# A DRAM scratch laid out chunk by chunk, and tiles re-paired so that each partition's copy is one run

## What is computed

```python
x0 = xk = e                                   # (B, 39, 16), e from 39 gathers
for idx, (W, b) in enumerate([(w0, b0), (w1, b1), (w2, b2)]):
    z = jnp.einsum('bhd,bkd,hks->bsd', x0, xk, W) + b[None, :, None]
    z = jax.nn.relu(z)                        # (B, 128, 16)
    if idx != 2:
        xk = z[:, :64, :]; direct.append(z[:, 64:, :])
    else:
        direct.append(z)
logit = jnp.sum(jnp.concatenate(direct, axis=1), axis=-1)
h = jnp.concatenate([logit, dense_ctx], axis=1)
h = relu(h @ W_top1 + b_top1); h = relu(h @ W_top2 + b_top2); y = h @ W_top3
```

## Time and profile before

| | us |
|---|---|
| median of 3 runs | 2626.11 |
| lowest and highest | 2624.89, 2628.14 |
| span of the profiled execution | 2627.2 |
| PE busy | 2462.9 (94%) |
| DVE busy | 2273.2 (87%) |
| POOL busy | 1559.0 (59%) |
| ACT busy | 1176.3 (45%) |
| SP's DMA queue, share of 16 engines | 88.7% |

### The profile page before, as it was taken

How to read it: one execution, slowest core, us unless ns; L and a number is a source line. 1 busy time by engine, 2 the same in 40 slices (tenths; PEclk the granted TensorE clock), 3 DMA queues, 4 the chain that set the end, 5 groups by cost and what they waited for, 6 DMA issues and landing times.

```text
span 2627.2 us, 25816 instructions
## 1 busy us (share of the span) xinstructions
PE 2462.9 (94%) x7712; PEld 1439.5 (55%) x7712; DVE 2273.2 (87%) x1356; ACT 1176.3 (45%) x1414; POOL 1559.0 (59%) x1030
## 2 busy tenths in 40 slices
PE   0399999999999999999999999999999999999999
PEld 0155555555555555555555555555555555555553
DVE  0389989898998999899999989999898999989970
ACT  0144444444444444444444444444444444444442
POOL 6456666576666656665765666566566656732340
PEclk9899999999999999999999999999999999999999
DMA  2999999999999999999999999999999999999920
GB/s 61 182 200 201 200 185 197 193 193 186 200 198 188 194 192 199 189 194 196 191 196 186 202 190 194 193 194 195 184 200 185 198 194 197 194 187 196 194 47 0
DMA packets 262599, 477.02 MB, mean 182 GB/s; under 512 B 19371, under 2 KB 37675, under 8 KB 262501
## 3 DMA queue, kind: packets, MB, share of 16 engines
q1 hardware_dynamic: 242102, 471.34, 88.7%
q0 software_dynamic: 20480, 5.47, 1.7%
HBM read 468.99 MB, written 7.74 MB: 181 GB/s over the span
## 4 chain that ended last, share of the span: by engine, by line
PE 67%; POOL 10%; issue 7%; DMA 6%; DVE 6%; ACT 2%; SPq 1%; POOLq 0%; DVEq 0%; ACTq 0%
PE z L647 34%; PE z L670 29%; POOL emb L339 5%; DMA emb<-in_tbl,idx 5%; DVE prod L406 4%; POOL pair_lo L210 4%; PE xk L729 1%; DMA x_pairs<-x_transposed 1%; PE z L729 1%; ACT pair_hi L520 1%; PE turned L628 1%; POOL half_parts L206 1%; DVE logit L436 1%; DVE pair_lo L210 1%; ACT direct L581 0%
## 5 line engine op out<-in xcount | busy, mean ns | idle before, releaser
L406 DVE TENSOR_TENSOR prod<-x_pairs,xk 128x2048 f32<-128x2048 f32 x640 | 1439.5, 2282 | 142.3 <-PE z L670 107.0
L647 PE MATMUL z<-prod,w_plain 128*128 128x512 f32 (+2 forms) x2944 | 1401.5, 600 | 48.7 <-issue 27.0
L520 ACT CAST pair_hi<-prod 128x1024 fp32r<-128x1024 f32 x703 | 735.5, 1046 | 1122.3 <-PE z L670 780.6
L210 POOL TENSOR_TENSOR pair_lo<-prod,pair_hi 128x1024 fp32r<-128x1024 f32 x320 | 763.5, 2386 | 679.3 <-ACT pair_hi L520 663.9
L647 PEld LDWEIGHTS z<-prod,w_plain 128*128 128x128 f32 (+2 forms) x2944 | 561.6, 191 | 488.6 <-issue 407.7
L339 POOL DMA_INDIRECT emb<-in_tbl,idx x624 | 702.2, 1125 | 189.3 <-issue 176.6
L670 PE MATMUL z<-pair_hi,w_lo 128*128 128x512 f32 (+1 forms) x1408 | 793.2, 563 | 2.6 <-DVE pair_lo L210 1.7
L670 PE MATMUL z<-pair_lo,w_hi 128*128 128x512 f32 (+1 forms) x1408 | 556.8, 395 | 0.0
L670 PE MATMUL z<-pair_hi,w_hi 128*128 128x512 f32 (+1 forms) x1408 | 556.1, 395 | 0.0
L210 DVE TENSOR_TENSOR pair_lo<-prod,pair_hi 128x1024 fp32r<-128x1024 f32 (+1 forms) x384 | 468.1, 1219 | 49.5 <-ACT pair_hi L520 48.7
L670 PEld LDWEIGHTS z<-pair_hi,w_lo 128*128 128x128 f32 (+1 forms) x1408 | 267.0, 190 | 300.4 <-POOL pair_lo L210 139.9
(11 more groups left out here) (50 smaller groups left out, 567.0 us busy)
## 6 DMA issues: line engine op xcount, KB each, us to landing
x_pairs<-x_transposed SPq DMA_DIRECT2D x128, 2432.0 KB
x_diag<-x_transposed SPq DMA_DIRECT2D x192, 546.0 KB
x_pairs<-x_transposed SPq DMA_DIRECT2D x64, 256.0 KB
x_diag<-x_transposed SPq DMA_DIRECT2D x192, 78.0 KB
emb<-in_tbl,idx POOLq DMA_INDIRECT x624
x_transposed<-stage SPq DMA_DIRECT2D x32, 156.0 KB
x_transposed<-stage SPq DMA_DIRECT2D x32, 80.0 KB
x_pairs<-in_w SPq DMA_DIRECT2D x2, 704.0 KB, 7.0
```

The costliest lines, as they stand in the source:

```text
L210: engine.tensor_tensor(pair_lo[0:rows, pair % PAIR_RING], held[0:rows, at:at + 2, :], pair_hi[0:rows, pair % PAIR_RING].bitcast(F32), ALU. ...
L406: nc.vector.tensor_tensor(prod[0:rows, pos % RING, 0:n, :], a, xk.unsqueeze(1).broadcast_to([rows, n, N]), ALU.mult).then_inc(prod_ready, 1)
L520: nc.scalar.copy(pair_hi[0:rows, pair % PAIR_RING], held[:, at:at + 2, :]).then_inc(hi_ready, 1)
L647: ins = nc.tensor.matmul(z[n][:], w, held[0:rows, i, :], start=(k == 0 and i == plain[0]), stop=(k == last_slot and not here and i == plai ...
```

## The change

- The scratch becomes `[64 chunks, 59 x 512]`: a row is a chunk, and in it the fields stand one behind the other, 2 KB each, 118 KB in all. The store has the same shapes and piece sizes (1 KB).
- `x0_diag`: band i, tile t, partition f holds field f + 7i + t, in place of f + 3t + i. A partition's seven pieces are now one run of 14 KB.
- `x0_pairs`: tile t holds field t on partitions 0 to 63 and field t + 19 on 64 to 127. Each partition's 19 pieces are one run of 38 KB.
- The weights are paired to match. The host function is the same text, but with other constants (`DIAG` 1, `T0` 21, `PLAIN_TILES` 0 to 18) it lays `w0` out as 39 rows of 21 tiles and `w1`, `w2` as 20 tiles in their natural order. SP picks the halves: layer 0's two arrays with three DMAs each, layers 1 and 2 with one DMA per half tile (64 partitions x 128 values, 512 bytes a partition), and one each for the last tile.

```diff
-    xt = nc.dram_tensor("x0_transposed", [F + WRAP, COLS], F32, kind="Internal").ap()
+    xt = nc.dram_tensor("x0_transposed", [GROUPS * CHUNKS, (F + WRAP) * N], F32, kind="Internal").ap()
...
-            sp.dma_start(w0_swapped, w0s).then_inc(swapped_in, 16)
-            sp.dma_start(w0_raw, w0f).then_inc(swapped_in, 16)
-            plain = [len(PLAIN_TILES[n]) for n in (1, 2)]
-            for raw, w, first in zip(w_raw[1:], (w1, w2), plain):
-                sp.dma_start(raw.rearrange("p (t s) -> p t s", s=S), w[:, first:]).then_inc(raw_in, 16)
-            loads = [(w_plain[1][:], w1[:, 0:plain[0]]), (w_plain[2][:], w2[:, 0:plain[1]]),
...
+            for dst, src in ((w0_swapped, w0s), (w0_raw, w0f)):
+                for i in range(BANDS):
+                    sp.dma_start(dst[i * F:(i + 1) * F], src[:, i * TILES0 * S:(i + 1) * TILES0 * S]
+                                 ).then_inc(swapped_in, 16)
+            def load_rows(dst, w, tiles, loaded):
+                for half in range(2):
+                    rows = slice(half * HALF, (half + 1) * HALF)
+                    for at, t in enumerate(tiles):
+                        h = t + half * (TX - 1)
+                        sp.dma_start(dst[rows, at], w[h % 2 * HALF:(h % 2 + 1) * HALF, h // 2]
+                                     ).then_inc(loaded, 16)
+            for raw, w, n in zip(w_raw[1:], (w1, w2), (1, 2)):
+                raw = raw.rearrange("p (t s) -> p t s", s=S)
+                load_rows(raw, w, SPLIT[n], raw_in)
+                sp.dma_start(raw[:, W_SPLITS[n] - 1], w[:, TX - 1]).then_inc(raw_in, 16)
+            for dst, w, n in zip(w_plain[1:], (w1, w2), (1, 2)):
+                load_rows(dst[:], w, PLAIN[n], weights_in)
+            sp.dma_start(columns[:], small).then_inc(weights_in, 16)
...
-                    shifted = bass.AP(tensor=chunk.tensor, offset=chunk[i:i + F].offset,
-                                      ap=[[COLS, F], [DIAG * COLS, T0], [1, N]])
-                    sp.dma_start(x0_diag[rows, 0:T0, :], shifted).then_inc(x0_diag_in, 16)
+                    shifted = bass.AP(tensor=chunk.tensor, offset=chunk[:, i * TILES0 * N:].offset,
+                                      ap=[[N, F], [1, TILES0 * N]])
+                    sp.dma_start(x0_diag[rows, 0:TILES0, :].rearrange("p t n -> p (t n)"), shifted
+                                 ).then_inc(x0_diag_in, 16)
...
-                    src = chunk[half:half + F - 1].rearrange("(t two) n -> t two n", two=2)[:, 0, :]
-                    sp.dma_start(buf[half * HALF:(half + 1) * HALF, 0:TX - 1, :],
-                                 src.partition_broadcast(HALF)).then_inc(loaded, 16)
+                    src = chunk[:, half * (TX - 1) * N:(half + 1) * (TX - 1) * N]
+                    sp.dma_start(buf[half * HALF:(half + 1) * HALF, 0:TX - 1, :]
+                                 .rearrange("p t n -> p (t n)"),
+                                 src.rearrange("o n -> (o n)").partition_broadcast(HALF)
+                                 ).then_inc(loaded, 16)
```

More of the change, by code:

```diff
@@ L49 @@
 RING = 4
-SL0, SLX = -(-T0 // QUAD), TX // QUAD
+SL0, SLX = -(-TILES0 // QUAD), TX // QUAD
 SLC = SL0 + 2 * SLX
-L0_FIRST = range(0, T0, QUAD)
+L0_FIRST = range(0, TILES0, QUAD)
 FIRST_TILE = (0, 4, 16, 8, 12)
@@ L66 @@
 assert CHUNKS * sum(PAIRS.values()) % PAIR_RING == 0
-SPLIT_TILES = {n: [(FIRST_TILE if n else L0_FIRST)[k] + at + i
+SPLIT = {n: [(FIRST_TILE if n else L0_FIRST)[k] + at + i
                    for k, at, m in SPLITS[n] for i in range(m) if m == 2] for n in SPLITS}
-PLAIN_TILES = {n: [t for t in range(TX - 1 if n else T0) if t not in SPLIT_TILES[n]] for n in SPLITS}
+PLAIN = {n: [t for t in range(TX - 1 if n else TILES0) if t not in SPLIT[n]] for n in SPLITS}
 W_ORDER = (1, 2, 0)
-W_SPLITS = {n: len(SPLIT_TILES[n]) + (n > 0) for n in SPLITS}
-X0_DIAG_DMAS, X0_PAIRS_DMAS, ST_DMAS = 2 * DIAG, 3, 4
-RAW_DMAS, WEIGHT_DMAS, TOP_DMAS = 2, 3, 6
+DIAG, T0, R0 = 1, BANDS * TILES0, F
+PLAIN_TILES = {n: list(range(TX - 1)) for n in (1, 2)}
+SPLIT_TILES = {n: [] for n in (1, 2)}
+W_SPLITS = {n: len(SPLIT[n]) + (n > 0) for n in SPLITS}
+X0_DIAG_DMAS, X0_PAIRS_DMAS, ST_DMAS = 2 * BANDS, 3, 4
+TOP_DMAS = 6
+RAW_DMAS = sum(2 * len(SPLIT[n]) + 1 for n in (1, 2))
+WEIGHT_DMAS = sum(2 * len(PLAIN[n]) for n in (1, 2)) + 1
 H1, H2, DENSE = 512, 256, 16
@@ L130, in build @@
         ident = sb("ident", [P, P])
-        w_plain = [sb(f"w{n}_plain", [P, len(PLAIN_TILES[n]), S]) for n in SPLITS]
+        w_plain = [sb(f"w{n}_plain", [P, len(PLAIN[n]), S]) for n in SPLITS]
         w_hi = [sb(f"w{n}_hi", [P, W_SPLITS[n], S], F32R) for n in SPLITS]
@@ L201, in low_part @@
         def low_part(engine, layer, pos, at, n, pair):
-            held, rows = prod[:, pos % RING], P if layer else R0
+            held, rows = prod[:, pos % RING], P if layer else ROWS0
             if n == 1:
@@ L248, in load_chunk @@
             def load_chunk(bt, c):
-                first = ahead(bt * (P * D) + c * N)
+                first = ahead(bt * CHUNKS + c)
                 sums = bt * CHUNKS + c
@@ L261, in load_chunk @@
                     sp.wait_ge(summed2, sums)
[L262 to L263 removed]
+                chunk = xt[bass.ds(first, 1), :]
+                base = chunk[:, 0:F * N].rearrange("o (f n) -> (o f) n", n=N)
+                for i in range(BANDS):
                     rows = slice(i * F, (i + 1) * F)
[L266 to L269 removed]
+                    shifted = bass.AP(tensor=chunk.tensor, offset=chunk[:, i * TILES0 * N:].offset,
+                                      ap=[[N, F], [1, TILES0 * N]])
+                    sp.dma_start(x0_diag[rows, 0:TILES0, :].rearrange("p t n -> p (t n)"), shifted
+                                 ).then_inc(x0_diag_in, 16)
+                    sp.dma_start(x0_diag[rows, TILES0, :], base).then_inc(x0_diag_in, 16)
                 if not (isinstance(bt, int) and bt == c == 0):
@@ L416, in products @@
                         dve.wait_ge(xk0_ready, next_chunk + 1)
-                    first, rows, tiles = (FIRST_TILE[k], P, TX) if n else (L0_FIRST[k], R0, T0)
+                    first, rows, tiles = (FIRST_TILE[k], P, TX) if n else (L0_FIRST[k], ROWS0, TILES0)
                     product(slot, pos, copies[0:rows, first:min(first + QUAD, tiles), :], xk[0:rows])
@@ L640, in layer @@
                     here = [s for s in splits if s[0] == k]
-                    places = range(QUAD if n else min(QUAD, T0 - t))
+                    places = range(QUAD if n else min(QUAD, TILES0 - t))
                     plain = [i for i in places if not any(at <= i < at + m for _, at, m in here)]
@@ L644, in layer @@
                     for i in plain:
-                        rows = P if n else R0_LAST if t + i == T0 - 1 else R0
-                        w = whole[0:rows, PLAIN_TILES[n].index(t + i), :]
+                        rows = P if n else ROWS0_LAST if t + i == TILES0 - 1 else ROWS0
+                        w = whole[0:rows, PLAIN[n].index(t + i), :]
                         ins = nc.tensor.matmul(z[n][:], w, held[0:rows, i, :],
@@ L661, in layer @@
                             for i in range(2):
-                                j = SPLIT_TILES[n].index(t + at + i)
-                                rows = P if n else R0
+                                j = SPLIT[n].index(t + at + i)
+                                rows = P if n else ROWS0
                                 p_hi = pair_hi[0:rows, pair % PAIR_RING, i, :]
```

37 lines of the change are left out of this document (15 added, 22 removed).

## The result

| | before | after |
|---|---|---|
| median, us | 2625.5 (4 runs, 2623.77 to 2628.14) | 2928.95 (4 runs, 2920.93 to 2934.69) |
| ratio | | 1.1155, 95% interval 1.1129 to 1.1182 |
| span of the profiled execution | 2627.2 | 2932.9 |
| mean granted clock | 0.982 | 0.949 |

The account below looks back on a forecast made before the run. PE was taken as the bound, with DMA costing time only in the start and at 15 group turns, through gathers behind x0 loads. 2627.2 - 21 - 72 = 2534, less 1.1 to the median, 2533 us; range 2524 to 2615, chance 0.79.

Parts of the forecast that it names:

- I take 395, the row of long runs: x0 loads: with runs of 14 and 38 KB they would move at 395 GB/s, like the weights.
- The lower bound, 205: x0 loads: the lowest rate allowed for, 205 GB/s, meaning no change.
- Part 2: Group turns: x0_pairs is in before the last gather, so PE's wait and clock dip go; 4.8 x 15 = 72 us gained.
- Part 1: Start: the first chunk's loads come in sooner; 21 us gained, bounds 0 and 23, up to 5 more for the clock.
- the 2 us that I gave ACT's "remote" wait: Start: ACT's wait, taken as a fetch sharing the DMA engines that ends when they are free, given 2 us.
- layer 0's copies were to be in at 76.0: Start: layer 0's 1872 KB at 395 GB/s would be in at 76.0, so layer 0 is no obstacle.
- Part 3: Start: 85 weight DMAs on SP take 39 us, covered by the gathers until 60.5; at 1.04 each, 26 us lost.
- I take 0.45, near the small one: Start: SP's time per small weight DMA, 0.45 us, so 39 us for all 85.
- Part 4: Store pieces, padding, DVE's products and matmuls keep their shapes: no effect on the time.
- Rival 4: Group turns: gathers starve behind 38 KB pieces, 3.0 us each; PE waits 4 us longer 15 times; 2686 us, chance 0.15.
- Rival 3: Start and turns: nothing changes, since reading one place from 16 engines is the limit; 2626 us, chance 0.06.
- rivals 1 and 2: x0 loads: rate rises partway, 250 GB/s, 2583 us, chance 0.15; only piece overhead goes, +4.7%, 2609 us, chance 0.06.

Follow-up runs that it names:

- e5: Kernel before, with x0_pairs read in 2 KB pieces from an embedding table, each of the 64 partitions from its own place: 2616.32 us.
- e6: Kernel before, with x0_pairs read in 2 KB pieces from an embedding table, all 64 partitions reading the same 19 pieces: 2628.70 us.
- e1: Changed kernel, with 256 B of nothing behind each field in the scratch, so that copies are 2 KB pieces again: 2643.84 us.
- e15: Kernel before, its two x0_pairs DMAs writing even and odd partitions in place of lower and upper 64: 2547.73 us.
- e9: Kernel before, x0_pairs loaded by one DMA over 128 partitions in place of two over 64, same 2 KB pieces for all: 2542.44 us.
- e10: e3 with x0_pairs loaded by one DMA over 128 partitions in runs of 38 KB, the same for all: 2544.00 us.
- e11: Kernel before, with ACT issuing the upper half of x0_pairs on its own queue from the second chunk on: 2620.82 us, ratio 0.9991.
- e3: Changed kernel, with the weights laid out by the host so that seven DMAs load them again in place of 85: 2908.49 us.
- e7: Kernel before, each large x0_pairs DMA cut in two by columns, giving 1 KB pieces: 2627.43 us, ratio 1.0004.
- e16: Kernel before, x0_pairs loaded by 38 DMAs of one field each, lower and upper half by turns: 2612.20 us.
- e18: Kernel before, x0_pairs loaded by ten DMAs of up to four fields, lower and upper half by turns: 2604.07 us, ratio 0.9915.
- e8: Kernel before, each large x0_pairs DMA cut in four by columns, giving 512 B pieces: 2732.85 us.

## Why the prediction was wrong

**The step that failed: "I take 395, the row of long runs."** The sum needed the rate of `x0_pairs`, and I had rows at 205, 174, 395 and 316. I put their difference down to where the pieces stand in DRAM. But those rows differ in a second thing, which partitions are written: the weights go to 117 or 128, `x0_pairs` to 64 neighbours. The columns of the profile show the shapes, and I did not hold them against the rates. e5, e6 and e1 change where the pieces stand, at 215, 210 and no gain; e15 changes the partitions alone and gets 383. The page of the Trainium skill that I drew on was the one on small descriptors; the one that bore on the case was "SBUF — State Buffer". The lower bound, 205, was the truth, and the point value stood at the wrong end. The prediction also called the engines full in the `x0_diag` part; its own row has 0.89 there, beside 174 GB/s.

**Parts 1 and 2** hung on that rate. Where it holds, in e9 and e10, they can be read apart:

- Part 2, 72 us at the turns: e9 has 147.24 us per group against the 147.7 forecast, and no wait at the turns. That is 5.3 us a turn and 79 in all, somewhat more than the 4.8 and 72 of the sum. Right.
- Part 1, 21 us in the start: e9's first product from `x_pairs` starts at 105.57, so 7 us. The step that failed there is the 2 us that I gave ACT's "remote" wait. In e9 it is 15.9 us, as it was before (15.56); it isn't a transfer that the faster load sets free. What ACT waits for I can't name; three kernels (after, e1 and e11) don't show the wait. A second term was off too: layer 0's copies were to be in at 76.0, by 395 GB/s in `x0_diag`. With runs of 14 KB and the old start (e3) they came at 85.77, against 86.42 before.
- Together 2542.4 for e9 against 2533. So the mechanism behind the turns was right, and this change doesn't touch it.

**Part 3**, the weights: the step that failed is "I take 0.45, near the small one". Over all 85 it was 1.05 us, so the last was through at 90.1: the upper bound, 1.04 and 89, was the truth, and the last 36 with 1.4 each were beyond it. From 40 to 88 the DMA engines are busy 16% of the time only, so it isn't their rate. Cost: 19 (e1) or 20 us (e3) by the times, 14 or 23 by the first product, inside the 26 that I gave as that part's end.

**Part 4** was right: ACT's busy time is as before, 1176.6, and DVE's within 0.5%.

**Rival 4**, with its 0.15, is what happened, and at 3.0 us a turn. Its size at a turn was right too: 4 us more per turn forecast, 7.06 - 3.08 = 3.98 measured. Its price was 60 us in 15 turns, and the loss is 306. The step that failed is that it counted the gathers' users at the turns only. POOL waits for its gathers ahead of *every* chunk's `pair_lo`, which "The kernel before" says in so many words, and the profile before showed 9.1 us from gather to work where a gather took 8.9. Add it: 60 at the turns, 172 behind `pair_lo`, 52 for the clock, 23 in the start. Its condition, a rate below 286 GB/s, was right, and 209 was far below it. The Trainium skill's rule on arbitration ("DMA: Bandwidth & Descriptors", section "Queues, rings and completion order"), that an engine changes queues only between packets, is borne out at 38 KB: within the load the gathers land no more packets than SP's queue does, one engine's turn being 3.0 us, and 240 of 320 packets land behind it. Between 1 and 2 KB e7 shows no such dependence, so it isn't what made the 8.9 us of the kernel before.

**Rival 3** (nothing changes) was right about the rate for a wrong reason; rivals 1 and 2 did not occur. The range ended at 2615 because it left rivals 3 and 4 out; rival 4's own figure, 2686, would not have reached 2929 either.

**What stays open.** What ACT's "remote" wait is. Why blocks by turns reach 220 to 287 GB/s in e16 but 200 to 245 in e18, and whether a better split of the halves gets all of e9's 83 us in a kernel that computes the reference: e9's and e15's placement of the fields would need other tiles of `xk` and other weights, and I did not build that. Why the `x0_diag` loads, 39 partitions each, stay near 170 GB/s with runs of 2 or of 14 KB. Whether the small weight DMAs cost 1.4 us because of their number, their 512 bytes or the gathers beside them was not tried apart.

## What to carry to other kernels

Compare the rates of two DMAs only when they write the same partitions: here a transfer into 64 neighbouring partitions stayed at 205 to 215 GB/s with pieces from 1 to 38 KB, and went to 383 when its partitions were spread. Before making pieces longer, look for a small transfer on another queue that is waited for, list *every* wait on it, and take the slack at each from the trace; 38 KB pieces turned a slack of about 0.2 us (an estimate) into 4.4 us lost per chunk. Long pieces are harmless where the load is through before anyone waits (e10), and a loss where it isn't.

## What the runs showed of the hardware that I had not expected

- One packet can be a whole run of 38,912 bytes, which takes 3.0 us at 209 GB/s, and gathers on another queue then get at most about one packet per turn.
- Two DMAs that write every other partition run at 383 GB/s, one after the other, with 64 partitions each. It is the choice of partitions, not their number.
- Two queues that write opposite halves move about 320 GB/s while both have work (e11), but the second one's data set in some 8 us after the first's, with its issue only 2.9 us later.
- Pieces of 1 KB cost nothing against 2 KB (e7, ratio 1.0004), those of 512 bytes 4% of the kernel (e8, a single run).
- 36 DMAs of 64 x 512 bytes took SP 50 us in after and 45 in e1, 1.4 and 1.25 each, with the DMA engines 16% busy; the first 20 took 0.63 each.
